# A cosformer attention block with a mixture of experts on one core: the expert stage in plain f32 on 39 blocks of 128 rows

## What is computed

```python
x = L0_attn_x                                     # 1 x 2048 x 128
x = x + attn(layernorm(x), Wq, bq, Wk, bk, Wv, bv, Wo, bo)   # 16 heads of 64, causal, cosformer
y = layernorm(x)                                  # xf: 2048 rows of 128
logits = xf @ gate_w                              # 8 experts
top_w, top_idx = top_k(logits, 2)
top_w = softmax(top_w)
combine = zeros(t, 8).at[arange(t)[:, None], top_idx].add(top_w)
h = gelu(einsum('td,edf->tef', xf, w1) + b1)      # 128 -> 512, exact gelu
y = einsum('tef,efd->ted', h, w2) + b2            # 512 -> 128
out = x + einsum('ted,te->td', y, combine)
```

## Time and profile before

| | us |
|---|---|
| median of 3 runs | 428.3 (426.67 to 430.45) |
| profiled execution, its own time | 427.45 |
| its span in the profile | 425.6 |
| PE busy | 372.6 (88%) |
| DVE busy | 290.7 (68%) |
| ACT busy | 182.5 (43%) |
| POOL busy | 149.2 (35%) |

### The profile page before, as it was taken

One profiled execution on the slowest core, in us unless ns is written; L12 is line 12 of the kernel. 1 busy time (PEld: TensorE's weight loads), 2 busy tenths in 40 slices (PEclk: granted clock), 3 DMA queues, 4 the chain that ended last, 5 costly groups with the idle time before them and its releaser, 6 DMA issues.

```text
span 425.6 us, 10824 instructions
## 1 busy us (share of the span) xinstructions
PE 372.6 (88%) x4183; PEld 333.3 (78%) x4183; DVE 290.7 (68%) x774; ACT 182.5 (43%) x400; POOL 149.2 (35%) x141
## 2 busy tenths in 40 slices
PE   2999999999988999998899998889985589999910
PEld 1878899879877888987888897778875589999810
DVE  5688676798664667866566888456881558888805
ACT  4673333672212366221246633124650456666600
POOL 2022533050452102055211317743357234655530
PEclk9999999999998999999999999999998599999985
DMA  7702977949110099001000101234343545678119
GB/s 259 203 2 58 235 193 191 150 115 187 27 33 14 8 165 142 17 29 31 10 8 2 49 22 51 76 84 137 113 122 123 140 141 150 196 204 230 59 47 249
DMA packets 50210, 45.46 MB, mean 107 GB/s; under 512 B 5155, under 2 KB 43616, under 8 KB 50160
## 3 DMA queue, kind: packets, MB, share of 16 engines
q1 hardware_dynamic: 44416, 38.94, 39.1%
q0 software_dynamic: 2496, 4.24, 3.0%
q10 hardware_dynamic: 3248, 1.60, 1.4%
HBM read 26.61 MB, written 19.06 MB: 107 GB/s over the span
## 4 chain that ended last, share of the span: by engine, by line
PE 67%; DVE 8%; issue 7%; another core or an unknown queue 5%; ACT 5%; POOL 3%; DMA 3%; ACTq 0%; POOLq 0%; DVEq 0%
PE ps L1365 7%; PE ps L1400 7%; PE ps L1239 7%; PE ps L1241 6%; PE ps L1240 6%; PE ps L1372 6%; PE ps L1344 6%; PE ps L1327 6%; PE ps L1574 5%; PE ps L1392 3%; ACT hT L738 2%; PE ps L1284 2%; DMA zin<-zbuf 2%; PE ps L1577 2%
## 5 line engine op out<-in xcount | busy, mean ns | idle before, releaser
L693 ACT ACTIVATE os<-ps 128x260 f32<-128x260 f32 x64 | 24.9, 389 | 114.6 <-PE ps L1372 97.6
L495 POOL TENSOR_TENSOR on<-tcs,rden 128x1024 f32<-128x1024 f32 x16 | 30.5, 1904 | 91.1 <-DVE rden L926 91.1
L578 POOL DMA_INDIRECT zbuf<-z,yb x46 | 46.6, 1012 | 43.8 <-DVE z L1155 35.9
L913 DVE TENSOR_TENSOR state<-ps,state 128x260 f32<-128x260 f32 x64 | 27.3, 427 | 44.4 <-ACT os L693 41.0
L1574 PE MATMUL ps<-W,hT_hi 128*128 x176 | 45.4, 348 | 7.1 <-DVE z L1155 6.0
L1365 PE MATMUL ps<-vcs,am 128*64 128x65 f32 x1024 | 44.8, 228 | 2.6 <-issue 2.5
L903 DVE TENSOR_TENSOR am<-ps,pair 128x1024 f32<-128x1024 f32 x32 | 38.9, 1215 | 10.2 <-issue 6.4
L1365 PEld LDWEIGHTS ps<-vcs,am 128*64 128x64 f32 x1024 | 38.4, 140 | 7.7 <-issue 3.8
L738 ACT ACTIVATE hT<-ps,w1b 128x256 f32<-128x256 f32 x92 | 36.2, 477 | 19.0 <-PE ps L1241 10.0
L1327 PE MATMUL ps<-qT,kT 64*128 64x128 f32 x512 | 39.5, 287 | 3.9 <-issue 3.4
L1574 PEld LDWEIGHTS ps<-W,hT_hi 128*128 128x128 f32 x176 | 34.5, 196 | 9.5 <-issue 9.2
(11 more groups left out here) (147 smaller groups left out, 843.2 us busy)
## 6 DMA issues: line engine op xcount, KB each, us to landing
w1b<-w1s SPq DMA_DIRECT2D x23, 514.0 KB
ybuf<-blank SPq DMA_DIRECT2D x16, 520.0 KB, 9.0
win<-in_L_ffn_w SPq DMA_DIRECT2D x16, 256.0 KB, 3.5
w1s<-W SPq DMA_DIRECT2D x8, 512.0 KB, 4.5
yb<-ybuf SPq DMA_DIRECT2D x23, 130.0 KB
x_sb<-in_L_attn_x SPq DMA_DIRECT2D x4, 256.0 KB, 4.9
pair<-c_pair SPq DMA_DIRECT2D x16, 64.0 KB, 2.0
zin<-zbuf SPq DMA_DIRECT2D x4, 256.0 KB, 5.8
```

The lines of the kernel that those rows point to most:

```text
L578: pool.indirect_dma_start(zbuf, bass.IndirectOffsetOnAxis(ap=yb[b % YR][:, h, D:D + 1].bitcast(U32), axis=0), z[:, b % ZR, h, :], None, bo ...
```

## The change

The split into high and low parts is gone from the expert stage: rows, hidden values and both sets of weights are used as plain f32, and one matmul takes the place of three (or of two). Blocks have 128 rows, and there are 39 of them. The first weights are read from the input by expert (256 KB a block, six buffers), the second weights lie as f32 in `w2_sb`, loaded in the last group's attention. The bias columns no longer travel with the weights: for every block the table's matmuls pick a row of `b1q` and give the column `b1t` (four matmuls more in each `block_table`). There are two tables: 17 blocks are sure to be full when three groups are known, the other 22 come at the end. The blank rows are made on POOL and written in 8 large transfers. POOL writes each block's result with one indirect DMA, and the first three results before the last unit's rows. `YR`, `ZR`, `WR`, `XR` are the numbers of buffers for rows, results, first weights and turned rows.

```diff
-TB = 2 * P
+TB = P
-TABLES = (2, 3, 4)
-FIRST = (0, full_after(T - SC * P), full_after(T - 2 * P))
+TABLES = (2, 4)
+FIRST = (0, full_after(T - SC * P))
 NB = (2 * T + E * (TB - 1)) // TB
-YR, ZR = 8, 6
+YR, ZR, WR, XR = 10, 8, 6, 4
...
+            def load_block(b):
+
                 if b >= YR:
-                    sp.wait_ge(z_out[(b - YR) % ZR], 32 * ((b - YR) // ZR + 1))
+                    sp.wait_ge(z_out[(b - YR) % ZR], 16 * ((b - YR) // ZR + 1))
                 at = sp.value_load(tab[0:1, 1, b:b + 1], min_val=0, max_val=PLACES)
+                sp.dma_start(yb[b % YR][:], ybuf[bass.ds(at, TB), :]).then_inc(yb_in[b % YR], 16)
+                if b >= WR:
+                    sp.wait_ge(h_ps, 2 * (b - WR) + 2)
+                sp.dma_start(w1b[b % WR][:], w1[bass.ds(at // PITCH, 1), :, :].rearrange("e p n -> p (e n)")
+                             ).then_inc(w1_in[b % WR], 16)
...
+            first_root(0)
+            pool.memset(state[:], 0.0).then_inc(memsets, 1)
+            pool.memset(blank[:], 0.0).then_inc(memsets, 1)
...
             second_rows(NS)
+            for b in range(3):
+                results_out(b)
             for m in range(4):
                 rows_out(NS, m)
-            for b in range(NB - 1):
+            for b in range(3, NB):
                 results_out(b)
...
                 if b >= 2:
-                    act.wait_ge(hlo_ok, 2 * (b - 1))
+                    act.wait_ge(z_ps, b - 1)
...
+            def block_rows(b):
+                dve.wait_ge(xb_ps, b - 1)
+                dve.tensor_copy(xb[:, b % XR, :], ps[:, 5, b % 2 * P:b % 2 * P + P]).then_inc(xb_ok, 1)
+
+            def weighed(b):
+
+                dve.wait_ge(z_ps, b + 1)
                 if b >= ZR:
+                    dve.wait_ge(z_out[b % ZR], 16 * (b // ZR))
+                dve.tensor_scalar(z[:, b % ZR, :], ps[:, 4, 0:D], yb[b % YR][:, D + 1:D + 2], None, ALU.mult
+                                  ).then_inc(z_ok, 1)
...
                 n = COUNT[t]
                 pe.wait_ge(match_ok, t + 1)
+                pe.wait_ge(b1_in, 16 * E)
+                for f in range(FB):
+                    mm(ps[:, bank, 352 + f * n:352 + (f + 1) * n], b1q[:, f * P:(f + 1) * P], match[:, 0:n],
+                       start=True, stop=True, skip_group_check=True)
...
+                    last = mm(ps[:, b % 2 * 2 + f // 2, f % 2 * P:f % 2 * P + P], w1b[b % WR][:, f * P:(f + 1) * P],
+                              xb[:, b % XR, :], start=True, stop=True, skip_group_check=True)
...
+                    w = w2_sb[:, bass.ds(which, 1), f * D:(f + 1) * D].rearrange("p e n -> p (e n)")
+                    last = mm(ps[:, 4, 0:D], hT[:, b % 2, f, :], w, start=(f == 0), stop=(f == FB - 1))
                 last.then_inc(z_ps, 1)
+
+            def step(b):
+                if b + 2 < NB:
+                    block_rows(b + 2)
+                if b + 1 < NB:
+                    hidden(b + 1)
+                down(b)
```

More of the change, by code:

```diff
@@ L197, in moe_block @@
         attn.close()
[L198 to L204, removed]
+        w2_sb = sb("w2_sb", [P, E, F])
+        w1b += [sb(f"w1b{k}", [P, F]) for k in range(2, WR)]
         zin = sb("zin", [P, 2, NC, D])
+        hT = sb("hT", [P, 2, FB, P])
+        yb += [sb(f"yb{k}", [P, ROW]) for k in range(3, YR)]
+        z = sb("z", [P, ZR, D])
         x_in = [sem(f"x_in{k}") for k in range(NS)]
@@ L211, in moe_block @@
         wl_in = [sem(f"wl_in{k}") for k in range(3)]
[L212 to L215, removed]
+        w1_in = [sem(f"w1_in{k}") for k in range(WR)]
+        w2_in = sem("w2_in")
+        b1_in = sem("b1_in")
         yb_in = [sem(f"yb_in{k}") for k in range(YR)]
@@ L218, in moe_block @@
         zin_in = [sem(f"zin_in{k}") for k in range(NS)]
-        blank_in = sem("blank_in")
-        blank_out = [sem(f"blank_out{k}") for k in range(NS)]
+        tri_in = sem("tri_in")
+        blank_out = sem("blank_out")
         y_out = [sem(f"y_out{k}") for k in range(NU)]
@@ L354, in _ @@
             sp.dma_start(wo_sb[:], Wo.rearrange("(b p) n -> p b n", p=P)).then_inc(c_in, 16)
[L356 to L375, removed]
+            sp.dma_start(on[:, 1, 0:4, :], c_tri.rearrange("p s (h d) -> p (s h) d", d=DH)).then_inc(tri_in, 16)
+            sp.dma_start(ids[:], c_ids).then_inc(tri_in, 16)
             def pair_in_next(i, c):
@@ L418, in _ @@
-            sp.wait_ge(bias_out, 16)
-            for k in range(2):
-                sp.wait_ge(stage_out[k], 16 * E // 2)
-            def load_weights(b):
-                if b >= 3:
-                    sp.wait_ge(h_ok, (b - 2) * FB)
-                which = sp.value_load(tab[0:1, 0, b:b + 1], min_val=0, max_val=E - 1)
-                sp.dma_start(f32(w1b[b % 3][:]), w1s[bass.ds(which, 1), :, :].rearrange("e p n -> p (e n)")
-                             ).then_inc(w1_in[b % 3], 16)
-            def load_rows(b):
+                blank_next(2 + c)
@@ new lines, in _ @@
+            for e in range(6, E):
+                sp.wait_ge(big_ps, QK_JOBS + 2 + 6 * (e - 6))
+                blank_next(e)
+            sp.dma_start(ybuf[PLACES:PLACES + TB, :], blank[:, 0, :]).then_inc(blank_out, 16)
+            for e in range(E):
+                sp.dma_start(b1q[e * QC // E:(e + 1) * QC // E, :], b1[e:e + 1, :].broadcast_to([QC // E, F])
+                             ).then_inc(b1_in, 16)
+            for i in (1, 2):
+                for c in range(SC):
+                    pair_in_next(i, c)
@@ L1461, in first_rows @@
                     pe.wait_ge(yb_in[b], 16)
-                    for h in range(2):
-                        last = pe.transpose(ps[:, 6, b * TB + h * P:b * TB + h * P + P], yb[b][:, h, 0:D], ident[:])
+                    last = pe.transpose(ps[:, 6, b * P:b * P + P], yb[b][:, 0:D], ident[:])
                 last.then_inc(xT_ps, 1)
```

533 lines of the change are left out of this document (157 added, 376 removed).

## The result

The changed kernel takes 415.0 us (median of 4 runs, 414.4 to 416.3) where the kernel before takes 427.5 beside it: a ratio of 0.970 (0.965 to 0.9755), faster by 3.0%. The forecast was 422.0, 1.3% under the profiled 427.45 that it was summed on. The profiled execution took 414.4 us with a span of 412.5, so 13.05 us less than the profiled 427.45.

A forecast was written before the change was run, and what follows sets the result against it. The prediction took the kernel to be bound by TensorE, with one hole near 325 us. Terms +1.0 - 2.0 - 0.5 - 1.7 - 2.2 = -5.4 took 427.45 to 422.0 us, range 408 to 431.

The forecast's parts named there:

- blocks: Expert stage, steady PE work: 39 blocks of 2.09 us, 81.5 against 80.5 before, so +1.0 us.
- hole: PE idle near 325 us and half clock behind it: 11.0 us expected for 13.2, so -2.2 us.
- rest of the expert stage: Projection, gates, tables and small waits: 18.0 us, +1.0 for bias columns, -3 for waits gone, so -2.0 us.
- attention: Stage up to 295.2 us: -1.5 for lighter POOL and ACT, +1.0 for bias columns, blank rows 0, so -0.5 us.
- end: Behind the last matmul: DVE and one POOL issue replace ACT, DVE, POOL and two issues, -1.7 us.
- lower bound of 2.00: Lowest PE time of a new block, from the b2 rows' 8 recorded matmuls: 78.0 us in all, -2.5 us.
- reading (b): Expert stage's idle PE: a long unbroken run of POOL's indirect DMAs goes with a stand of PE's signals until it ends.
- Rival 1: The idle stretch near 325 us closes, giving 411 us; chance 0.30.
- Rivals 2 and 3: Second: PE's register load shows per block, 434 us, chance 0.12; third: longer POOL run, PE stands 17 us, 428, chance 0.08.

The follow-up runs named there:

- the kernel before with late pauses: Kernel before with a POOL memset behind each indirect DMA of the last two row units and the first six blocks' results: 420.5 us, ratio 0.984.
- the pauses: Changed kernel with POOL memsets between indirect DMAs: behind last two row units and results 0 to 8, 409.4 us; between all, 387.8 us.

## Why the prediction was wrong

The terms of the sum against the two profiled executions, each cut at the same points of the program:

| term | predicted | measured |
|---|---|---|
| blocks | +1.0 | 39 x 1.895 - 80.5 = -6.6 |
| hole | -2.2 | 11.2 - 13.2 = -2.0 |
| rest of the expert stage | -2.0 | (96.9 - 73.9 - 11.2) - 18.0 = -6.2 |
| attention | -0.5 | +3.4 |
| end | -1.7 | 17.0 - 18.7 = -1.7 |
| sum | -5.4 | -13.1 |

**Blocks: the step that failed.** It was "The projection is of just this shape: 16 recorded matmuls (8 in the code) from 282.18 to 284.17, 1.99 us". Shape and count were right, but I measured to the start of the next group, and this distance depends on both neighbours: at 282.18 matmuls of 64 columns stand before the projection and matmuls of 64 rows behind it. Two other projections of the kernel before are shorter. The first has the 64 columns before it and 128-row transposes behind, the second 128 rows and columns on both sides:

```profile
61.01 2.05 PE L1400 MATMUL ps<-wo_sb,oT 128*128 128x128 f32 x16
62.90 0.60 PE L1246 MATMUL ps<-ident,xh 128*128 128x128 f32 x4
...
79.83 1.95 PE L1400 MATMUL ps<-wo_sb,oT 128*128 128x128 f32 x16
81.62 0.60 PE L1284 MATMUL ps<-ident,kT 128*128 128x128 f32 x4
```

They take 1.89 and 1.79 us, and the changed kernel's 0.90 + 0.89 are the same 1.79. A step of 1.895 for 2.09 is 7.6 us over 39 blocks. That this nearly equals the 7.7 by which the forecast missed is luck: the rest (-4.2) and the attention (+3.9) missed too, and cancelled. My lower bound of 2.00 came from such a distance as well, 0.95, which I had read as 0.96; the same group takes 0.89 at 160.86 in the kernel before and in the changed kernel. So the bound did not hold either. Why it is 0.95 there, with 128-row transposes behind it, the rows don't show. The four passes of "FP8 and Floating Point Precision" (TensorE Precision Notes) in the Trainium skill, 1.71 us by estimate, stood nearer to 1.79 than my row; I had dismissed it for the row. The trace agrees within 5%.

**Attention: a cost taken at nothing, and a fall of the clock that the change did not make.** POOL's blank rows had been given "0 to +3; I take 0, as DVE has to be hit on its critical operation". It was hit. Timeline at the start, changed kernel, then the kernel before:

```profile
6.32 0.95 POOL L423 MEMSET state<- 128x1040 f32 x1
6.38 3.31 DVE L678 TENSOR_SCALAR xh<-x_sb,mv,rstd 128x128 f32<-128x128 f32 x4 [1.24 <-POOL rstd L419]
...
7.22 1.82 POOL L424 MEMSET blank<- 128x2080 f32 x1
...
9.18 1.11 PE L1066 MATMUL ps<-ident,xh 128*128 128x128 f32 x4 [3.11 <-DVE xh L678]
```

```profile
6.68 0.85 DVE L829 TENSOR_SCALAR xh<-x_sb,mv,rstd 128x128 f32<-128x128 f32 x3
6.82 1.24 PE L1246 MATMUL ps<-ident,xh 128*128 128x128 f32 x4 [0.22 <-DVE xh L829]
```

POOL clears `state` (0.95 us, before the change at 0.77 us of the span) and then the blank rows (1.82) beside DVE's four scalings, which take 3.31 us instead of 1.11. PE's first large matmul comes at 11.80 instead of 9.57, +2.2. No run moved these memsets; that they are the cause is read from the rows.

The stretch between two projections that holds the first table (from 267.29 to 285.48, before from 267.73 to 282.18) is 3.7 us longer where I had +1.0. Without stands it takes 12.3 us with the bias columns and 11.3 in the kernel before, so the columns are worth the 1.0, and the rest is the half clock behind the stand. That rest is not the change's: in the profiled execution of the kernel before with late pauses, where the clock fell as well, the stretch takes 17.1 us and the attention 298.0. Against this execution the change costs the stretch 1.1 us and the whole attention 0.6, where I had said -0.5. So most of the +3.4 is a matter of which execution was profiled, and most of the +3.9 by which this term seems to have missed. What is left, some -2.5 for POOL's and ACT's lighter load where I took -1.5, is a remainder that no run measured alone.

**Rest.** The waits that went were not only those within a block: PE's waits of 1.4 us for `z` ahead of the last half block and 1.2 for `combT` are gone as well. They are 2.6 of the 4.2 us between -2.0 and -6.2; where the other 1.6 went is not shown.

**The hole** was right in mechanism, by reading (b), and in size, though it came in two pieces. That the size came out is partly luck: of its two parts the idle time was 5.5 where I had 7.5, the clock 5.7 for 3.5. Rival 1, the closed hole, named 411; the time came near it for another reason. Its page ("SBUF — State Buffer", SBUF: two separate sides, in the Trainium skill) says that DVE's f32 copies within SBUF keep GpSimd from writing its DMAs' descriptors. The changed kernel has 11.2 us of holes with most of those copies gone, and the pauses remove them with DVE's work unchanged: the runs speak against that rule as their cause. Rivals 2 and 3 did not occur.

**What the forecast never asked** is the largest finding. It took a steady 9 tenths of PE in the attention as bound by PE. Reading (b), which it held, says that every run of four transfers holds PE, and the row at 129.25 is one of them; the six together, with the clock behind them, cost 16 to 17 us in both kernels.

## What to carry to other kernels

Measure a group's time to a neighbour of the same shape, or better from several copies of it; one distance can hold the change from and to another kind of work, and 0.2 us a block became 8 us. Before a difference between two profiled executions is put down to a change, see whether another execution of the same program has it too: one fall of the clock made 2.6 us here. When a mechanism is found in one place, sum it over all places where its conditions hold, also in stretches that look busy. On POOL, try to spread indirect DMAs out: a break of 0.70 us between them gave 5% to 6% in kernels whose PE read 9 tenths busy nearly everywhere. The price is POOL's time, which must stay under that of the step it serves.

## What the runs showed of the hardware

- While POOL issues indirect DMAs (0.97 us each, 128 rows of 512 or 520 bytes) 0.30 us apart, PE's issue and the signals of PE and of landed transfers stand, by up to some 4.7 us (`h_ps` #9). DVE's and ACT's own operations do not lengthen: a scaling takes 0.35 us at 328.04 within such a run, as behind it at 336.26, two Gelus take 0.63 at 329.56 within it, and four 1.14 at 336.88 behind it, both 0.26 us a Gelu after the first. Breaks of 0.30, 0.39, 0.49 and 0.70 us gave 415, 416.5, 410 and 385 us. Whether the break or the mean rate counts, and which resource is shared, stays open.
- The hold doesn't depend on where PE's 16,384-byte instruction loads fall: moved out of POOL's second run and into its first, they left stands of 1.67 and 2.34 us where 1.72 and 2.12 had been.
- Behind such a stand the granted clock falls to half, 1.2 GHz, for 6 to 7 us in three places of the changed kernel (0.50, 0.53 and 0.52 in the windows), but not in every execution: behind the stand at 278 us the kernel before had 1.00 in one execution and 0.50 in another of the same program up to there.
- A plain f32 matmul of 128x128 by 128 columns takes 0.22 us in a steady row, as two records of 0.11. Eight of them, to the start of the next group, take 1.79, 1.89 or 1.98 us by what stands before and behind.
- POOL memsets of 0.95 and 1.82 us beside DVE's four scalings went with 3.31 us for these where the kernel before takes 1.11.
